# Two products instead of three for the attention's denominators: high and low key sums side by side as 44 stationary columns

## The reference, cut to what matters

```python
q = jax.nn.elu(q) + 1.0
k = jax.nn.elu(k) + 1.0
kv = jnp.einsum('bhsd,bhse->bhde', k, v)
z = 1.0 / jnp.einsum('bhsd,bhd->bhs', q, k.sum(axis=-2))
out = jnp.einsum('bhde,bhsd,bhs->bhse', kv, q, z)
```

## Time and profile before

| | us |
|---|---|
| median of 3 executions | 1904.53 (1902.96 to 1904.88) |
| profiled execution, its own time | 1903.6 |
| its span | 1901.9 |
| TensorE busy | 1851.5 (97% of the span) |
| VectorE busy | 1296.5 (68%) |
| GpSimd busy | 558.1 (29%) |

### The profile page before, as it was taken

One profiled execution on the slowest core, in us unless ns is written; L12 is line 12 of the kernel. 1 busy time (PEld: TensorE's weight loads), 2 busy tenths in 40 slices (PEclk: granted clock), 3 DMA queues, 4 the chain that ended last, 5 costly groups with the idle time before them and its releaser, 6 DMA issues.

```text
span 1901.9 us, 28584 instructions
## 1 busy us (share of the span) xinstructions
PE 1851.5 (97%) x10824; PEld 1758.4 (92%) x10824; DVE 1296.5 (68%) x2242; ACT 654.5 (34%) x1243; POOL 558.1 (29%) x441
## 2 busy tenths in 40 slices
PE   6999999999899999999999999999999999999998
PEld 4678999999899999989999999999999999999998
DVE  7987579998894323878796654454558966465548
ACT  6534238887884411225211111111341111211113
POOL 1000001210001132214355654444024455455420
PEclk9999999999999999999999999999999999999999
DMA  5433302122244210033311111111240111111314
GB/s 166 123 117 103 104 14 59 44 58 60 70 142 140 67 50 1 26 98 106 97 41 34 34 50 34 51 48 56 80 139 26 34 50 35 50 34 34 112 47 125
DMA packets 83133, 131.17 MB, mean 69 GB/s; under 512 B 7462, under 2 KB 53320, under 8 KB 82990
## 3 DMA queue, kind: packets, MB, share of 16 engines
q1 hardware_dynamic: 78430, 115.97, 20.8%
q10 hardware_dynamic: 4560, 13.31, 2.3%
HBM read 101.06 MB, written 28.20 MB: 68 GB/s over the span
## 4 chain that ended last, share of the span: by engine, by line
PE 86%; DVE 5%; ACT 5%; issue 3%; ACTq 0%; SPq 0%; DVEq 0%; DMA 0%
PE pb L809 20%; PE pa L809 17%; PE pb L1304 11%; PE pb L1284 9%; PE pa L870 5%; PE pb L1314 5%; PE pb L947 3%; PE pa L1029 3%; PE pb L1190 3%; PE pa L983 2%; PE pb L1029 2%; ACT sm L1787 1%; PE pb L817 1%; PE pb L1065 1%; ACT o1h L1813 1%
## 5 line engine op out<-in xcount | busy, mean ns | idle before, releaser
L809 PE MATMUL pa<-dw_hi,hh 128*125 128x384 f32 x608 | 156.8, 339 | 1.7 <-issue 1.1
L809 PE MATMUL pa<-dw_hi,hl 128*125 128x384 f32 x608 | 156.0, 338 | 0.0
L809 PE MATMUL pa<-dw_lo,hh 128*125 128x384 f32 x608 | 155.6, 337 | 0.0
L2713 DVE TENSOR_TENSOR hl<-tr,hh 128x448 fp32r<-128x448 f32 x144 | 152.1, 1056 | 5.0
L2711 DVE CAST hh<-tr 128x448 fp32r<-128x448 f32 x144 | 78.7, 546 | 88.2 <-ACT tr L2047 83.0
L2081 ACT ACTIVATE cp<-pb 128x448 f32<-128x448 f32 x32 | 17.4, 544 | 323.1 <-PE pb L1304 316.4
L2047 ACT ACTIVATE tr<-pb,V 128x448 f32<-128x448 f32 (+1 forms) x96 | 57.1, 597 | 198.7 <-PE pb L1284 142.1
L1492 POOL CAST dw_hi<-raw 128x768 fp32r<-128x768 f32 x48 | 49.2, 1025 | 230.7 <-PE pa L809 228.5
L870 PE MATMUL pa<-S1h,D1h 125*125 125x418 bf16 x510 | 103.4, 356 | 8.1 <-DVE S1h L2207 8.1
L809 PEld LDWEIGHTS pa<-dw_hi,hh 128*125 128x125 f32 x608 | 108.8, 185 | 2.2 <-issue 1.3
L809 PEld LDWEIGHTS pa<-dw_lo,hh 128*125 128x125 f32 x608 | 109.6, 185 | 0.0
(11 more groups left out here) (470 smaller groups left out, 5134.7 us busy)
## 6 DMA issues: line engine op xcount, KB each, us to landing
raw<-in_L_mix_fc_w SPq DMA_DIRECT2D x48, 384.0 KB, 3.4
raw<-in_L_ffn_w SPq DMA_DIRECT2D x47, 384.0 KB, 3.4
md<-md_d SPq DMA_DIRECT2D x11, 546.9 KB
md_d<-mds SPq DMA_DIRECT2D x10, 546.9 KB
raw<-in_L_mix_qkv_w SPq DMA_DIRECT2D x24, 192.0 KB, 4.2
md<-md_d ACTq DMA_DIRECT2D x8, 546.9 KB
TOK<-in_x SPq DMA_DIRECT2D x10, 336.0 KB
xn_d<-TOK SPq DMA_DIRECT2D x10, 336.0 KB
```

The source lines that it names most:

```text
L809: last = nc.tensor.matmul(slot[:, c, :], x_[:, cols], w_[:, c * HD2:(c + 1) * HD2], start=(k == 0 and n == 0), stop=(k == len(blocks) - 1 ...
L2713: v.tensor_tensor(hb_lo[b][:, o:o + w], z, hb_hi[b][:, o:o + w].bitcast(fp32), ALU.subtract).then_inc(sem("h_lo"), 1)
```

## The change

The high and the low key sums now stand in one tile `kd_both` of 44 columns: the high parts in columns 0 to 11, zeros in 12 to 31, the low parts in 32 to 43. One product of all 44 columns with the high queries gives high times high in rows 0 to 11 of PSUM and low times high in rows 32 to 43. A second product of the first 12 columns with the low queries adds to rows 0 to 11. VectorE copies rows 32 to 43 into `zr`, adds rows 0 to 11, and takes the reciprocal of the sum from SBUF. GpSimd sets the 20 columns between to zero once, long ahead.

```diff
-                  + [ ("kd", [P, KT, NHEAD], fp32), ("kd_hi", [P, KT, NHEAD], f32r), ("kd_lo", [P, KT, NHEAD], f32r),
+                  + [ ("kd", [P, KT, NHEAD], fp32), ("kd_both", [P, KT, ZLOW + NHEAD], f32r),
...
-                for n, (w_, x_) in enumerate(((RE["kd_hi"], qh), (RE["kd_hi"], ql), (RE["kd_lo"], qh))):
-                    last = nc.tensor.matmul(pa[0:NHEAD, 1 + c % 2, 0:w], w_[:, m, :], x_, start=(m == 0 and n == 0), stop=(m == KT - 1 and n == 2))
+                for n, (rows, x_) in enumerate(((ZLOW + NHEAD, qh), (NHEAD, ql))):
+                    last = nc.tensor.matmul(pa[0:rows, 1 + c % 2, 0:w], RE["kd_both"][:, m, 0:rows], x_, start=(m == 0 and n == 0),
+                                            stop=(m == KT - 1), skip_group_check=True)
...
+            g_.memset(RE["kd_both"][:, :, NHEAD:ZLOW].bitcast(fp32), 0.0)
...
-            ch.link(g_.tensor_copy(RE["kd_hi"][:], kd[:]))
-            g_.tensor_tensor(RE["kd_lo"][:], kd[:], RE["kd_hi"][:].bitcast(fp32), ALU.subtract)
+            kd_hi, kd_lo = RE["kd_both"][:, :, 0:NHEAD], RE["kd_both"][:, :, ZLOW:ZLOW + NHEAD]
+            ch.link(g_.tensor_copy(kd_hi, kd[:]))
+            g_.tensor_tensor(kd_lo, kd[:], kd_hi.bitcast(fp32), ALU.subtract)
...
-                ch.link(v.reciprocal(zr, pa[0:NHEAD, 1 + c % 2, 0:w]))
+                ch.link(v.tensor_copy(zr, pa[ZLOW:ZLOW + NHEAD, 1 + c % 2, 0:w]))
+                ch.link(v.tensor_tensor(zr, pa[0:NHEAD, 1 + c % 2, 0:w], zr, ALU.add))
+                ch.link(v.reciprocal(zr, zr))
```

## The result

The changed kernel takes 1909.69 us (median of 11 executions, 1906.65 to 1910.56), the kernel before 1904.65 (11 executions, 1902.96 to 1906.73). The ratio is 1.0024 with an interval of 1.0017 to 1.0032: 4.6 us slower, or 5.0 by the medians. The profiled execution took 1909.83 us, with a span of 1908.1.

A forecast was written before the change was run, and what follows sets the result against it. TensorE, 86% of the chain, was taken to bound the kernel. Chunk 0 (-1.33 + 2.7), chunk 1 (-0.76 + 2.05) and chunk 2 (-0.57 + 0.25) sum to +2.4 us: 1904.5 + 2.4 = 1906.9, range 1902.5 to 1909.5.

The forecast's parts named there:

- The price and the place of the products: Queries' stage: each saved product is worth 0.19 us, with 44 columns as with 12; 3.0 us at most.
- The added work: VectorE, ahead of each reciprocal: a copy and an addition reading PSUM, 1.23 us each time, not held by GpSimd.
- rival 5: VectorE's reciprocal, now reading SBUF, is held by GpSimd too: 4.2 us slower, 1908.7, chance 0.07.
- Both chunks held by GpSimd: Chunks 0 and 1: GpSimd holds VectorE's steps behind the reciprocal; TensorE waits 2.7 us ahead of den(0) and den(6).
- The tie of chunk 1: Chunk 1: GpSimd's split starts 0.2 us ahead of VectorE's cast, 2.05 us late net; otherwise 0.75.
- Chunk 2: Third place needing new factors: the subtraction ends 0.25 us late, the old hold by GpSimd's additions hiding the rest.
- the choice that the clock stays: TensorE keeps full clock behind the two new 2.7 us waits, so no clock loss enters the forecast.
- The likeliest case: Queries' stage: chunks 0 and 1 both held, clock stays; 2.4 us slower, 1906.9, chance 0.42.
- rival 1: TensorE's clock falls in the new waits, 1.7 us each: 1908.6 with one fall, 1910.3 with two; chance 0.18.
- Within 0.2%: Whole kernel: the time differs by no more than 3.8 us, what a measurement tells from no change; chance 0.75.
- rival 2: GpSimd doesn't get in the way of the factors; chunk 0 waits 0.85 us; 1.4 us faster, 1903.1, chance 0.13.
- Rival 3: Only chunk 0 is held by GpSimd, chunk 1 going the other way: 1.1 us slower, 1905.6, chance 0.15.

## Why the prediction was right or wrong

**The price and the place of the products: right.** 0.19 us each, 44 columns or 12, and a saving of 2.1 us of stage where nothing is added (the experiment's expectation was 2.4).

**The added work: right.** 0.58 and 0.58 us (L2612, L2613), 1.23 with the steps between. The reciprocal takes 2.74 us from SBUF, and 831.00 shows it undisturbed beside GpSimd. So rival 5 is out. The Trainium skill, VectorE: DVE Perf Modes, section Mode 2x_2P, would let a one-source instruction between SBUF tiles use both ports; for this reciprocal the trace doesn't bear that out, with 2.74 us from SBUF and 2.75 from PSUM.

**Both chunks held by GpSimd: right, and shown** by moving the splits and by the two single moves. Waits of 2.34 and 2.33 us that the profile records stand for delays of 2.48 and 2.5 against the 2.7 worked out; I had taken GpSimd's second instruction as 2.05 to 2.07 us long, and it took 1.81. The tie of chunk 1 went as forecast (GpSimd's CAST 0.21 us ahead of VectorE's), and the kernel with three products and the added work shows the other side of it.

**Chunk 2: right**, +0.23 for +0.25.

**What failed is the choice that the clock stays.** The likeliest case was 1906.9 with chance 0.42; what happened is rival 1, which had 0.18. The median of 1909.7 lies 0.2 above the end of the range; the ratio puts it at 1904.65 x 1.0024 = 1909.2, within. That it lies within is owed to the width of the range, which took in a fall and a half, and not to the sum. "Within 0.2%" had 0.75; the ratio of 1.0024 lies beyond that, and its interval, from 1.0017, on both sides. The sum without the clock was +2.4, and this execution shows +2.1; the clock brought 3.5 in it. The sentence at fault is "Against: a wait of 2.71 us at 41.69 is followed by ... full speed". It was one execution. The same place in the profile of the changed kernel, and the granted clock behind it:

```profile
41.92 11.87 PE L870 MATMUL pa<-S1h,D1h 125*125 125x418 bf16 x54 [2.72 <-DVE S1h L2210]
...
44.00:46.00 2.00, 2.00 (x7) 1.37 (x6) 2.00 (x7) 1.99 (x2) 0.00 (x0) 0.50 0.04 15
```

In the profiles of the changed kernel and of the ten experiments the same wait comes back, and ten of these eleven show a granted clock of 0.57 to 0.74 at 42 to 46 us. The row had shown the rarer outcome. For the new waits, 2.1 to 2.3 us long: a fall behind three of the five that aren't filled (den(0) and den(6) in the changed kernel, den(0) with only chunk 1's split later; none behind den(0) in the kernel before with the added work, none behind den(6) with only chunk 0's split later). Behind the wait of 2.6 to 3.2 us ahead of `q_apply(12)` it falls in all nine profiles without fillers there.

The Trainium skill, TensorE: Matmul & The Clock Gate, section HAM oscillation, which I had set against the change, describes the pattern: waits between bursts, with the cost of the clock paid again each time. Its example has waits of 3 to 5 us for a DMA; the runs here show it behind waits of 2.1 to 3.2 us, and behind the shorter ones not each time.

**Rivals 2 and 3** are what the experiments make of the kernel: rival 2's 1903.1 is the kernel with the splits later (1903.5), and its waits, 0.85 and, by its den(6) at 9.6, 0.5, are 0.72 and none that the profile shows. Rival 3's 1905.6 is the kernel with only chunk 1's split later (1905.8), but the agreement is in part chance: in its profile the clock fell behind den(0), which rival 3 leaves out.

## What to carry to other kernels

A saving of 0.19 us per product on the busiest engine was paid for with two small instructions in a chain whose slack was 0.6 us; before trading so, write down for each place where the chain is awaited when the result is wanted and when it comes, and which instruction of a third engine starts in between. A cast of VectorE from SBUF, or a subtraction with both inputs there, that stands in such a chain should not fall where GpSimd begins a long instruction; here GpSimd's work could be moved by one job at no cost (0.9996), and that took the whole loss away.

In these profiles a wait of 2.1 to 3.2 us on TensorE in this stage cost its length and, in 12 of 14 cases, a fall of the clock, some 1.6 us more behind the new waits. Take that as the likelier case, and don't let one profiled execution speak for the clock: the granted clock of every execution says more.

## What the runs showed of the hardware that was not expected

- The fall of the clock behind a wait isn't fixed by the wait: with 2.33 us ahead of den(6) the clock behind it was 0.51 and 0.64 in one kernel and 1.00 in another, and behind the wait at 42 us, ahead of anything that the edits touch, it fell in ten profiles and stayed in two. A wait of 2.0 us near 990 us, which all profiles have, was followed by a fall in two of twelve.
- VectorE and GpSimd take turns by whole instructions: a subtraction of 0.58 us, ready 0.2 us behind GpSimd's start, took 2.07 and ended 0.44 us behind GpSimd's end. In no row shown here did it get in ahead of that end.
